# Another order of the steps of a twelve-block kernel: one string replaced, every instruction kept

## The chip, the cores and the metric

The kernel runs on one core of one Trainium2 chip. The time is the device time of one execution in microseconds. It computes with TensorE (PE), VectorE (DVE), ScalarE (ACT) and GpSimd (POOL); SyncE (SP) issues the DMAs. Each engine takes its instructions strictly in the order in which they were written, and waits at semaphores for the others.

## The reference

A residual stream `x` of 64 sequences x 64 tokens x 128 channels runs through four layers of three blocks (cross attention over a context of 128 x 96 per sequence, self attention, feed-forward), all in fp32:

```python
x = x + _L0_xattn_ref(_layernorm(x), ctx_768, ...)   # L0x
x = x + _L0_attn_ref(_layernorm(x), ...)             # L0a: linear attention and an MLP
x = x + _L0_ffn_ref(_layernorm(x), ...)              # L0f: 16 experts, top 4
x = x + _L1_xattn_ref(ctx_768, _layernorm(x), mask, ...)   # L1x
...                                                  # L1a, L1f, L2x, L2a, L2f, L3x, L3a
x = x + _L3_ffn_ref(_layernorm(x), ...)              # L3f: 8 experts, top 2, and a shared one
return x
```

## The kernel before

The stream stays in SBUF for the whole run (`x_held`, 32 tiles of 128 tokens). A block is cut into jobs by groups of four tiles (two for L1x and L2f). Two contexts (0 and 1), each with its own four PSUM banks, SBUF rooms and semaphores, work on two jobs at a time; `PLAN` says which jobs each context does and in what order. Both contexts share the five engines.

A job's work on one engine is a Python generator: what stands between two `yield`s is one step, with its waits in front (`wait_ge`) and its semaphore increments behind. Each generator has a letter. Main programs: `p`, `c`, `m`, `n` on PE; `a`, `b`, `x`, `y` on ACT; `g` on POOL; `v`, `r`, `w`, `z` on DVE; `s` on SP. Early programs, of the context's next job while the present one runs: `d` on DVE (norm statistics), `l` on POOL, `k` on ACT, `q` on SP (context load). Small letters are context 0, capitals context 1. `ORDER` is one string; `write_out` walks along it and writes the next step of each letter's program. The relative order of letters of different engines has no effect on the chip; that of one engine is the order of its queue. A `+` loads the weights of the next block on SP, after a wait for the jobs that used the same room.

A digit in front of a PE letter sets `job.warm`: `pe_warm` (L471) then issues that many matmuls of constants, 128x512 in bf16, ahead of the step's wait. Nobody reads them; here they are called fillers.

Lines that the argument uses: L904, L908 and L914 are the gate, up and shared matmuls of the expert blocks and L946 their down matmuls; L893 is POOL's product with the experts' weights; L1596, L1606, L1624 and L1699 are matmuls of the attention of L1a and L3x and L1726 its reduction on DVE; L1976 and L1984 are the scores and the transposes of L2x, L2081 and L2087 its maximum and subtraction on DVE; L400 and L436 are the norm statistics of the early programs; L2786 adds the last block's result and L2809 stores it to `out`.

Of the kernel before, what the change touches and what calls it, by code (L numbers as in the profile page):

```python
# [3091 lines left out]
```

## Time and profile before

| | us |
|---|---|
| median of 3 runs | 2549.42 |
| the runs | 2548.19 to 2553.82 |
| profiled execution, its own time | 2545.65 |
| its span, first to last instruction | 2544.3 |
| PE busy / weight loads (PEld) busy | 2247.8 / 1508.2 |
| DVE / ACT / POOL busy | 1746.2 / 1371.3 / 775.2 |
| mean granted TensorE clock | 0.971 of full |

The profiled execution is 1.35 us longer than its span (what lies around it) and 3.8 us shorter than the median of the runs. A busy time is the union of an engine's instructions; the fillers count as busy. The idle time of a stretch is its length less the busy time.

### The profile page before, as it was taken

How to read it: one execution, taken by the hardware profiler on the slowest of the kernel's cores; microseconds unless marked ns; L12 is line 12 of the kernel's file. 1: busy time of each engine (PE TensorE's matmuls, PEld its weight loads, DVE VectorE, ACT ScalarE, POOL GpSimd, SP SyncE). 2: the span in 40 equal slices, each digit the busy share in tenths (PEclk: the TensorE clock that was granted, in tenths of full speed). 3: DMA queues.
4: the chain of work that ended last, by engine and by line, in shares of the span. 5: the costliest groups of instructions: out<-in, count | busy, mean ns of one | idle time of the engine just before them, and what ended most of it. 6: DMA issues, size and time to landing. Idle time of an engine off the chain costs nothing.

```text
span 2544.3 us, 62025 instructions
## 1 busy us (share of the span) xinstructions
PE 2247.8 (88%) x26402; PEld 1508.2 (59%) x26526; DVE 1746.2 (69%) x4832; ACT 1371.3 (54%) x2286; POOL 775.2 (30%) x676
## 2 busy tenths in 40 slices
PE   5989999878988888997888888898887889999999
PEld 3557666655565555565655676665555556556666
DVE  5766766677667777676777777777767675555642
ACT  4766567654554666544567544344454544555542
POOL 3333546433342212121222123211123223224543
PEclk9999999998999999999999999999998999999999
DMA  3011313200000000010000000000000102211232
GB/s 116 19 42 35 80 46 75 47 19 9 9 11 14 9 8 6 1 47 11 17 16 10 20 25 25 25 11 17 17 11 16 58 8 55 57 56 55 55 105 63
DMA packets 50453, 84.14 MB, mean 33 GB/s; under 512 B 9537, under 2 KB 24769, under 8 KB 49793
## 3 DMA queue, kind: packets, MB, share of 16 engines
q1 hardware_dynamic: 50176, 80.18, 11.5%
q8 instruction: 208, 3.41, 0.6%
q14 instruction: 69, 0.56, 0.1%
HBM read 77.54 MB, written 2.62 MB: 32 GB/s over the span
## 4 chain that ended last, share of the span: by engine, by line
PE 61%; DVE 24%; ACT 8%; issue 3%; POOL 2%; DMA 1%; SPq 0%; another core or an unknown queue 0%; DVEq 0%; POOLq 0%; ACTq 0%
PE psum L946 6%; PE psum L908 5%; PE psum L904 5%; PE psum L1606 3%; PE psum L463 2%; PE psum L471 2%; PE psum L1984 2%; PE psum L1699 2%; DVE c_L2x_mx L2081 2%; DVE c_L2x_p L2087 1%; DVE c_L3x_most L1726 1%; PE psum L1395 1%; PE psum L1596 1%; PE psum L1976 1%; PE psum L778 1%
## 5 line engine op out<-in xcount | busy, mean ns | idle before, releaser
L893 POOL TENSOR_TENSOR c_L3f_h<-c_L3f_h,c_L3f_spread 128x512 f32<-128x512 f32 x96 | 121.3, 1290 | 157.9 <-DMA c_L3f_spread<-scratch 91.6
L471 PE MATMUL psum<-halves_held 128*128 128x512 bf16 x438 | 129.4, 409 | 17.5 <-issue 9.8
L936 DVE TENSOR_TENSOR c_L3f_h<-c_L3f_h,psum 128x512 f32<-128x512 f32 (+1 forms) x112 | 76.0, 684 | 88.7 <-PE psum L908 63.1
L922 ACT ACTIVATE c_L3f_h<-psum 128x512 f32<-128x512 f32 (+1 forms) x112 | 65.8, 596 | 124.1 <-PE psum L904 117.5
L946 PEld LDWEIGHTS psum<-weights,c_L3f_h 128*128 128x128 f32 (+1 forms) x896 | 106.5, 191 | 19.5 <-issue 15.0
L946 PE MATMUL psum<-weights,c_L3f_h 128*128 128x128 f32 (+1 forms) x896 | 111.3, 278 | 0.3 <-POOL c_L3f_h L893 0.3
L904 PE MATMUL psum<-c_L3f_xT,weights 128*128 128x512 f32 x208 | 107.2, 600 | 0.2 <-DVE c_L3f_h L936 0.2
L908 PE MATMUL psum<-c_L3f_xT,weights 128*128 128x512 f32 x208 | 107.1, 601 | 0.0
L893 POOL TENSOR_TENSOR c_L0f_h<-c_L0f_h,c_L0f_spread 128x512 f32<-128x512 f32 x64 | 83.9, 1335 | 43.8 <-DVE c_L0f_h L936 32.5
L2020 ACT ACTIVATE c_L2x_p<-c_L2x_p 128x1024 f32<-128x1024 f32 x64 | 67.6, 1057 | 54.1 <-DVE c_L2x_p L2087 54.0
L1606 PE MATMUL psum<-c_L3x_qx,c_L3x_kT 32*128 32x256 f32 x512 | 75.3, 417 | 22.9 <-DVE c_L3x_most L1726 17.5
L471 PEld LDWEIGHTS psum<-halves_held 128*128 128x128 bf16 x558 | 51.3, 102 | 73.9 <-issue 33.1
L2081 DVE TENSOR_REDUCE c_L2x_mx<-psum 128x8 f32<-128x1024 f32 x64 | 77.9, 1220 | 19.4 <-PE psum L1976 18.7
L893 POOL TENSOR_TENSOR c_L2f_h<-c_L2f_h,c_L2f_spread 128x256 f32<-128x256 f32 x64 | 45.4, 735 | 143.4 <-DMA c_L2f_spread<-scratch 137.9
L1984 PE MATMUL psum<-constants_held,c_L2x_p 128*128 128x128 f32 x512 | 72.3, 289 | 13.3 <-ACT c_L2x_p L2022 13.1
L1984 PEld LDWEIGHTS psum<-constants_held,c_L2x_p 128*128 128x128 f32 x512 | 61.3, 149 | 30.3 <-issue 16.6
L2087 DVE SCALAR_TENSOR_TENSOR c_L2x_p<-psum,c_L2x_mx 128x1024 f32<-128x1024 f32 x64 | 78.0, 1221 | 1.3
L1726 DVE TENSOR_REDUCE c_L3x_most<-psum 128x16 f32<-128x2048 f32 x32 | 73.2, 2287 | 6.7 <-PE psum L1596 6.3
L1606 PEld LDWEIGHTS psum<-c_L3x_qx,c_L3x_kT 32*128 32x128 f32 x512 | 44.9, 191 | 50.9 <-DVE c_L3x_most L1726 25.8
L2025 ACT COPY c_L2x_pT<-psum 128x1024 f32<-128x1024 f32 x64 | 64.1, 1009 | 18.7 <-PE psum L1984 18.6
L1976 PE MATMUL psum<-c_L2x_kx,c_L2x_qT 32*64 32x512 f32 x512 | 62.8, 615 | 10.5 <-DVE c_L2x_va L2062 6.2
L922 ACT ACT_TABLE_LOAD x55 | 70.6, 1283 | 1.0
(640 smaller groups left out, 6514.1 us busy)
## 6 DMA issues: line engine op xcount, KB each, us to landing
c_L0f_spread<-scratch SPq DMA_DIRECT2D x64, 256.0 KB, 5.5
c_L3f_spread<-scratch SPq DMA_DIRECT2D x32, 512.0 KB, 5.5
c_L2f_spread<-scratch SPq DMA_DIRECT2D x64, 128.0 KB, 3.0
c_L3f_spread<-scratch SPq DMA_DIRECT2D x64, 128.0 KB, 5.9
c_L0x_ctxT<-ctxT SPq DMA_DIRECT2D x8, 384.0 KB, 7.7
c_L1x_ctx<-ctx SPq DMA_DIRECT2D x16, 192.0 KB, 2.4
c_L2x_ctxT<-ctxT SPq DMA_DIRECT2D x8, 384.0 KB, 3.6
c_L3x_ctxT<-ctxT SPq DMA_DIRECT2D x8, 384.0 KB, 3.6
```

The costliest lines, as they stand in the source:

```text
L471: nc.tensor.matmul(j.psum[:, bank, :], j.half["ident"], j.half["take"], start=True, stop=True)
L893: nc.gpsimd.tensor_tensor(h, h, j.m["spread"][:, f, :], ALU.mult).then_inc(*j.up("mixed"))
L904: t.matmul(psum[:, 1 + 2 * f % 3, 0:j.tok], j.weight("gate")[:, cols], m["xT"][:], start=True, stop=True).then_inc(*j.up("gate"))
L908: t.matmul(psum[:, 1 + (2 * f + 1) % 3, 0:j.tok], j.weight("up")[:, cols], m["xT"][:], start=True, stop=True).then_inc(*j.up("inner"))
L922: nc.scalar.activation(j.m["h"][P - rows:P, f, :], j.psum[0:rows, 1 + 2 * f % 3, 0:j.tok], ACT.Silu).then_inc(*j.up("silu"))
L946: put = nc.tensor.matmul(j.psum[:, 0, k * P:(k + 1) * P], j.m["h"][rows, f, k * P:(k + 1) * P], j.weight("down")[rows, f * P:(f + 1) * P], ...
L1606: nc.tensor.matmul(j.psum[rows, g, at:at + 256].rearrange("p (j q) -> p j q", j=QUAD), j.m["kT"][f, s * keys:(s + 1) * keys], j.m["qx"][f, ...
L1726: put = v.tensor_reduce(m["most"][:, u, :].rearrange("p (g j) -> p g j", j=QUAD), psum[:, :, u * QUAD * keys:(u + 1) * QUAD * keys].rearra ...
L1976: put = t.matmul(psum[64 * r:64 * r + 64, g, :].rearrange("p (j k) -> p j k", j=QUAD), m["qT"][f, s * S:(s + 1) * S], m["kx"][f, :, s * SC ...
L1984: put = t.transpose(psum[:, n // 4, (n % 4) * P:(n % 4 + 1) * P], m["p"][:, n * P:(n + 1) * P], j.c["ident"])
L2081: v.tensor_reduce(mx, s, AX, ALU.max).then_inc(*j.up(lane_name("max", h)))
L2087: v.scalar_tensor_tensor(p, s, -limit, bcast(mx, 2, SC), ALU.max, ALU.subtract).then_inc(*j.up(lane_name("low", h)))
```

## The change

The string `ORDER` is replaced by another of the same 8123 steps. The letters' counts are equal; the sum of the digits is 558 before and 590 after; they stand in front of 178 PE steps before and 189 after. `PLAN`, the programs, the tiles and every instruction except the fillers are the same. The first two, the 22nd and 23rd, and the last lines of the strings:

```diff
@@ -2838,76 +2838,76 @@
     "a2a3a4a5a6a7b3b4b5b6b7c3c4c5c6c7d8d9dadbdcdddedfe4e5e6e7f4f5f6f7g4g5g6g7h4h5h6h7i8i9iaibicidieifj4j5j6j7k5k6k7l6l7")

 ORDER = (
-    "vdDqDddldkqQdddplVDaL2pDaKQDdDDPpPagA1pgApLkpvGvD3PaAGvvVvpPaPKPg1paVAd5pagVdVdVPpAppvPlAlvda4PDAGQPGkvd5PvvD1PkVDpLVaAd"
-    "dDdvvlavdpavvaK1pVVvVP1PAApvvGkPvAlvG3PvQvvdPgPVvV9pgADDaDLaaVVaVPppppDapAppKDDDLDpQvvpPaAapaPaKpAPkdvvdvvdlGGvdlpvvPvPv"
...
-    "vAgpVKPpAPVPAvvvpPPAaPADqGPADVdpVADddvGvvalVavvVvGvvvvvvvvvvvvvLVp1PvaVDvpvAvPPdApAPapVvVpApvaVgVKppkvgPaApVaPvgpApvPgpV"
-    "+DPpVADp2PvvPVvVqpVVGPapPVGvVApVDvLagPv1pVaVPg3PdnAPzmAzzPwy6nwwAdPyVny2nVxVPdzlzV2mVG1nxVmzxmwzw3mzPyw7PwwAnxP3mynxymnx"
...
-    "PSPASpVPPAapVvpaGbPsLPAGPVDpvGsPaGApsVPGvPAsGPVPASgCVgCsPPASPVPApVCCpPpAGaPvGPVpAgaPKgPVvPGACVgPpGCaGACVgCCGCgCgCCCVSPpA"
-    "pPaPRvPRRgBRRpRRpRARvCgPBaSpApvSVPgPVSpAaPSvPVgPASGPVPAGPVGPAPGVPAGPVPGAPVGPAGPVPAGPVPGApVpGapvPaPvAPVPGAPVcAVcccccccccc"
-    "cccCvsCCCCCCCCCCCCCVS")
+    "dDddDDLDlqkKppaaPApaPAppp3PdqQDdvDQDddldLVggkGvDvaAGvvVvpPaPPgpaV3pAdagVdVVPpApKpvdPAlvaDdl2PAG5PkGv3PvdvDPDVpkQLVaDAddd"
+    "vvlva3plavvaKpVVvVPA3PApDDvvPGvAddvPvGvv2PgPvVQV8pAaaVVVPpppADapaLapgDpkppGKvDDvpPaAvaQv1pvaPvaAG2pkdddDPLvDlplvvdPvPvVk"
...
+    "gKpVPgAVpKPApPvVPPAvAvpPDADPaAdDGVddPqvAvpVGvaaVvVlvDvvvvvvvvvvvvGvvvVLpVDav1PvPAApvPvAKpaPVVpApVaVpvpgvapgPaApvdpVvgpPg"
+    "ApPVVpPDADpv2Pkv+PVPPvVVpVvVGaqppGVVDALvavPd1pgaVGnVPPzAzzPmwywAw3nAPPynyVVnVzzDPVxmVnxVmxmzwwz3mzPwwy7PwdA1nPxymnxymnxz"
...
+    "pVrrpVaVpVrpvDGapVpdvadpVPvApVrarpPbrPrArrApVcVbPvGAppGVaPsaPGKldPvvVPAppsAagAPgAsPgVcgcAcsgpgAPPsgPpAccaPcpPpappkpapapG"
+    "pKDVvVVVVvVVVVvDvvgpaVvpgVaDpVLcvPgVcgVcVgVcGcpVacvcVPVAcvVspaPApPAPGVArprapGVPrbPGDrrrvPrKVprPApPRRraPRRRpDBRpRvRPRDAPC"
+    "VAPVPApBcaaPVPvDAPbpvPVAPsVPSPpaPpvpapSAvpVGaPALPVASPsGVPGDAPVPGsApGpGPVPgvASPgVpPgASPagVCvgCGPpGapGCKAGPVCGCGCCCPACVCCc"
+    "CCCVvSPApapvPRRBRPRRRRPRRPACABpapvpVaPSVPAPVPAPVPAPSVpGPAPGVPGAPVPsSAPGVPAGPVPSgApgPVPSgvAPagVPsAcgPVGccGPGAcGccgPGVPcGC"
+    "GpgpaCAVCvCvCCCccCCCCCccccvCCVsS")
```

The last lines of the new string hold, for instance, `CCCccCCCCCccccvCCVsS` where the old one ends in `cccccccccccccCvsCCCCCCCCCCCCCVS`: the down steps of the two last L3f jobs alternate. In the 23rd line the first `n` (the first scores of L2x in context 0) stands ahead of two steps `P` of L1a instead of behind them.

## Rows read from the trace of the kernel before

**Rows 1.** The page's totals, and the span with the mean granted clock.
```profile
PE 2247.8 (88%) x26402; PEld 1508.2 (59%) x26526; DVE 1746.2 (69%) x4832; ACT 1371.3 (54%) x2286; POOL 775.2 (30%) x676
...
core 0: 2544.3 us, clock 0.971
```

**Rows 2.** Four stretches: busy us and instructions of each engine, PE's clock, DMA share, GB/s.
```profile
0.00:127.00 127.00, 95.79 (x641) 59.44 (x650) 84.34 (x252) 75.77 (x124) 45.32 (x40) 0.99 0.22 68
127.00:509.00 382.00, 354.23 (x2356) 246.64 (x2359) 255.62 (x935) 250.31 (x467) 172.21 (x137) 0.99 0.23 54
509.00:2162.00 1653.00, 1422.11 (x20511) 963.87 (x20624) 1204.78 (x3129) 861.60 (x1417) 414.88 (x386) 0.96 0.06 18
2162.00:2544.00 382.00, 375.71 (x2910) 238.24 (x2899) 201.49 (x520) 183.67 (x280) 142.82 (x113) 1.00 0.23 65
```

**Rows 3.** The same view, of the fillers (L471) alone, two stretches.
```profile
127.00:509.00 382.00, 2.72 (x8) 1.51 (x15) 0.99 0.23 54
509.00:2162.00 1653.00, 114.53 (x391) 45.30 (x496) 0.96 0.06 18
```

**Rows 4.** Chain that ended last: shares by engine, and by line.
```profile
PE 61%; DVE 24%; ACT 8%; issue 3%; POOL 2%; DMA 1%; SPq 0%; another core or an unknown queue 0%; DVEq 0%; POOLq 0%; ACTq 0%
...
by line: PE psum L946 6.4%; PE psum L908 5.2%; PE psum L904 5.1%; issue 3.3%; PE psum L1606 2.8%; PE psum L463 2.1%; PE psum L471 1.8%; PE psum L1984 1.7%; PE psum L1699 1.6%; DVE c_L2x_mx L2081 1.6%; DVE c_L2x_p L2087 1.3%; DVE c_L3x_most 
```

**Rows 5.** Who PE waited for: us in total, times, longest us.
```profile
PE psum L552 <- DMA c_L0x_ctxT<-ctxT: 22.0, 1, 22.0
```

**Rows 6.** Timeline 783 to 790: start us, us, engine, line, work, [idle before, releaser].
```profile
782.39 1.22 DVE L1726 TENSOR_REDUCE c_L1a_most<-psum 128x16 f32<-128x1024 f32 x1
783.09 0.69 ACT L480 ACTIVATE c_L2x_qT<-psum,weights 128x512 f32<-128x512 f32 x1 [2.74 <-PE psum L1897]
...
783.65 2.00 PE L1606 MATMUL psum<-c_L1a_qx,c_L1a_kT 32*64 32x256 f32 x24 [0.60 <-DVE c_L1a_most L1726]
...
785.57 0.87 DVE L400 BATCH_NORM_STATS2 c_L2x_norm_stats<-x_held 128x6 f32<-128x128 f32 x4
...
787.40 1.08 PE L1976 MATMUL psum<-c_L2x_kx,c_L2x_qT 32*64 32x512 f32 x4
...
788.99 1.23 DVE L2081 TENSOR_REDUCE c_L2x_mx<-psum 128x8 f32<-128x1024 f32 x1 [2.55 <-PE psum L1976]
```

**Rows 7.** Busy time of the engines from 783 to 795.
```profile
783.00:795.00 12.00, 9.92 (x158) 5.07 (x166) 8.77 (x19) 5.34 (x6) 2.12 (x2) 0.78 0.01 1
```

**Rows 8.** Timeline of PE from 1376 to 1381.
```profile
1377.02 2.78 PE L471 MATMUL psum<-halves_held 128*128 128x512 bf16 x8 [0.22 <-issue]
1379.63 1.58 PE L1984 MATMUL psum<-constants_held,c_L2x_p 128*128 128x128 f32 x13
```

**Rows 9.** The fillers: durations in ns (min/median/max), and their group (busy us, mean ns).
```profile
L471 PE MATMUL psum<-halves_held x438: 376/379/634, 25.6 to 2098.3; 128*128 128x512 bf16 x146
...
L471 PE MATMUL psum<-halves_held 128*128 128x512 bf16 x438 | 129.4, 409 | 17.5 <-issue 9.8 <-DVE c_L2x_p L2087 6.2
```

**Rows 10.** Timeline from 2499 to the end.
```profile
2499.21 0.19 PEld L908 LDWEIGHTS psum<-c_L3f_xT,weights 128*128 128x128 f32 x1 [0.24 <-issue]
...
2499.64 0.19 PEld L904 LDWEIGHTS psum<-c_L3f_xT,weights 128*128 128x128 f32 x1 [0.24 <-issue]
...
2515.52 25.75 PE L946 MATMUL psum<-weights,c_L3f_h 128*128 128x128 f32 x224
...
2528.42 0.69 DVE L2786 TENSOR_TENSOR x_held<-x_held,psum 128x512 f32<-128x512 f32 x1 [11.38 <-PE psum L946]
...
2541.31 0.69 DVE L2786 TENSOR_TENSOR x_held<-x_held,psum 128x512 f32<-128x512 f32 x1 [12.21 <-PE psum L946]
```

**Rows 11.** Weight loads on SP (to landing), and two starts, at 1693 and 1811.
```profile
DMA to landing us min/median/max: 2.6/4.3/11.4
...
1693.15 0.47 PE L2299 MATMUL psum<-c_L2f_klT,c_L2f_qlT 32*64 32x128 f32 x16
...
1811.18 0.87 DVE L436 BATCH_NORM_STATS2 c_L3a_norm_stats<-x_held 128x6 f32<-128x128 f32 x4
```

More of the change, by code:

```diff
@@ new lines @@
+    "AVlPVApVdApaPapVapaPVVkpVVpVpVVpvGvpVaG4pbPrrArprrrprrrrPdAPdrdrPKlPALADrPrArrPrrrrPaPVvVPcApbaVVAPsAVpVAppaPpsapPKDdDvv"
+    "DLVgVsgvpVVgDcVs+cVKgVcVapGspVcvPGApLpPgAPAPAPAPPaPavDPVgkVPpApaVVAPAVcVAcvpKDgvPgcVcvPVpVaVVpbVpVVrpraGpaVpv1PDGDArprrL"
+    "arrPrrLPdrrADPDrArrPArAvdPdrrrrPKrlPPcVbVPAppasPAAppApsaPpapsPKDDVVvVDVdLvLgVgvVgVcVsgcVpVgVsaVpGccVvcPvGApgapvgPDAPgPkP"
+    "AAPAPPKPVVPAcDA1PAcAcVVVVvpaPpbppaPpappKDDdVrrrrrrrdrrvrVrrrVdvrlrpaVpvrapVrdrpvDrrapcVVVbpvaGppLVavpsPGDApapPAPAPskPAgA"
@@ new lines @@
+    "PsgPKdPgvPsVgcvgcVsqcPDgDAdcgdcPlBcgdRRcdRRRcRRRDPRAvRPLPkdRVDRRPdRpRRaRPRdpqvapvRRAApVC+BaapgPalvSPVgPKvvAPVdAPVPAPgSVP"
+    "vAPGPppSvaVAPapGdVaSGCCGpSGCvGvCCGavCkGCvCVPdAdpavPlDBDdpdRaRRPRRpRkvpRadPRRpRRavpRRRpRRRdAdRRaRlapVPgaCvBgPAvPvVAPVdPSk"
+    "PgqAPvApvpadpaddDaPVlVSpPvGvPSGavdCLvPSA1pGavPGVkSpGaPApAGVdvppaaGDpvdapagqvpPaVCdgKCvGvCCCCgvCpvdpapaldaV1PkddApdvlv2PP"
+    "avPvdPBDRpRavRRRRRApRdaRRRPVpkvpapdvRaRRpdADDdaRpRRLaRVqRgpRvCaBPgAPlvvPVdAPdSdPVdAPgvPpvApaVpaaPSVpGPvvlPSaPvGvCSApGdad"
@@ new lines @@
+    "vCkSGCkGpAaCGpvppadDddaPvlVpVapGdqdKdGdapgCavCgCvvCVPADD1PgBPvRvDPR1pARpRaRLpaRRRaPlVARRRpkRPvRvdRPVRDRPaRRvRPRCvABVpavP"
+    "kpAaS3pvpavPddpddapldapVAgSvKpaGPaSGVPAdPgvPSGvAPVddCSqCgPvlApvpapaGdaPkGpGCvvVCVaCvGCvkpGavCpa2pvppdadddavplapagqpCaVPA"
+    "gvvdvPBdPddDPAQPgAPvlkpvRpdaRpRaVad3pPvvPVDRRRavPvRRRApaAvRPRRRRpkRDaVLpVvppavadpddDaRRpRRlRaDDgdpvDPaCBPgAvPvAVPKVPSPgP"
+    "v2pvpapaaAASVpPvGvSGaCvLCvSpGavCGDSkVpGDapGvCpdvGaCGpKpvCvCvCvVppgdPPVAgdVvPvPvQaAApAG+PvgAplvD2pGVaVDVpaapGVpdvvvV3pv7P"
@@ new lines @@
+    "AvpvDkpLPDaPADDApaPpaVVpAvvvDvVLVD9pDvpaPdKpVpKvAvPvAvPVg2PDApgPvPpvvdQadAlApPGAvgPvDDpVpALVaGpVVDaDDDappGvLVvdvD4pvk9Pv"
+    "pvV2pPaPAAApaPapVVpAvvvvDV9pVvpaPKVppKvApvPvAvPV1PgPDADAgvPvPpvdQadAVDApGLPgvDApvKV2pGaVVDdpDaapGVpvDvvLv3pl7PvpvdpVPaPA"
+    "AApaPapVVpAvvvkvVVD7pDvpaPdpVKApvPAvv2PvV1PPAgDDAppgvPvPvVDQaLAgpGvDPpKvAVpdaDApGaVVaDpDpvGvvLV4pv3PvdpvPlVpaPAAApaPapVV"
+    "pAvvvvDdVV9pkv1PApVadvvKvvpdaavPvvAvvv1PvvvVPPAvdvvAvvPvlvvDdPDpDDvaVvLADQAPpGvAvVGkVpVDaDpapGvDVpLVpPPgDAPvaAApgKpavPKp"
@@ new lines @@
+    "zdmwAwnlAPgzPKVzVV6mVz4PwwwVPAPyPPVnxVVymPVnVGdxDmDGxy2mVnwwzkVDzmLw2nwAwPzzxz9myVxV6nmyPxnmywPwnzAzpaPApvAdpdPaPvdqplVV"
+    "PvpVaV4pgaVGnVPPzmAzzdPAwDwPwyx8nAmyPnxyVnzzmVKVxVn1mzwz1PwzVPAm2PwyPVwnwynVPPVxyVVGmnDzzGxVnmVAzzx7mzwPw1myV1nwPwynwynV"
+    "zzDD3PxnLAmzgxPmAxmwAwz3mzPPwDwyw1nVVVx1PVymnxyVmnxVz2mzwwkpPaPApvKdpddPaAqpApPavPv2pgVaVlVmVnGwdw1PwzzzVPA2PPxPPV3myVx1"
+    "nVmVyxVGnmDyDwG2nwzzVnVA1mzPwzwzwyV7nxPVDPyLAmnGxmgxy1mw1nwzzkmPwwnAwPAPzzxz8mVVDVyPVxnmyxVnmyVPwnwzPzAmPwwAnwPAzPzxV6mz"
@@ new lines @@
+    "KVVVy2PxVnmy1PxnAy2m+wnVwzzDPDVpVAVaAVVVVV1pVVVVVVVDVvpVVaVpPpavApvPagVVVLVnVDmzzKPAzPwwPywAVPnGxPyVmndydGdxPAmnAzxzPmww"
+    "nVmzGPwzPzPVwPwGyPVxVVPnAmyDxDDVVPVmALAVnxVyV2mVlwnwVzzVVV1mVnwVwwzzxzdVVVVVVVV8mVPyA2nxPVmyxnmywVwkPAmnwzzwPAnwPzzxPzVP"
+    "VmGyAGPxnAgmyxPnyPmnzwwzPVpVaPGDpGvPKvpddadPVlVvVPAapvaDvVa2PvVVADAVVVVVVdVVVV6pVvVVVDVVVpPvVLvAVvPVpkaPpvpadAdPVvavpvaP"
+    "AVvPGPAVaPGPAVpGPvDPVpKvGdPvlvdPPpVaVVPA2pDkVvVPVpAAdVaVVVQVVVVVVVVVVVVV7pVVPAPVvvaavPVADDvPdadAPldVpGvPLAPVDpvvGvPAPpVa"
@@ new lines @@
+    "PVGkPpGKvpadPdPPVVvvpaVadVvlavlPDdDDdApvPpvGPvAv1pVa+QPAVpkvNpMapapYappXNagMYLNXkdZZZvWWWvvvvvvdMgXYpg2MNZZWWGdppppv7Nva"
+    "vpvMaZaWZpZpvvWvYvpvvNDvpvvK1pWYvNgYvvgvl8pXlaprrprbrrMrNrrrXvdrrrrrZcabMXpvpka1MpvsWpZWapMNWpWdapvspgWavsgcgcZgZcvcXcZv"
+    "paMpavapXppYvMvaXNgvYvpvMWWNgY1MgNZZpWWpWppvX3NkvaZvZpva2MaZpYpvXvNvvpYvMvXvNYMWNWZpZvPvA1pvPgvvgvdVPpAa2prrpdrbrrPGPrar"
+    "prrArprrarrdPcvvlbpvdppkaVAsVQNMZZpvapsZpgvasgvcgcWgcDcDWcYWvpaNYpavpXapMvvpXNgYMvlXNavMZZWWgvD2NMgZZpLpZpWDWpYWpvX6NvdY"
```

96 lines of the change are left out of this document (33 added, 63 removed).

## The prediction

> **What bounds the kernel now.** I read the totals first [rows 1]: TensorE (PE) is busy 2247.8 us of a 2544.3 us span, VectorE (DVE) 69%, nothing else over 54%. Those are averages, so the second view is the table of stretches [rows 2]. The reader should subtract PE's busy time from each stretch's length: 0 to 127 us leaves 31.2 us idle, 127 to 509 leaves 27.8, 509 to 2162 leaves 230.9, and the last 382 us leave 6.3. In 509 to 2162 DVE is busy 1204.8 of 1653 us (73%), so two engines take turns at being late; at both ends PE is alone. Third, the fillers: `pe_warm` (L471) issues matmuls nobody reads while PE would wait. They are counted as busy: 129.4 us in all, 114.5 of them in 509 to 2162 [rows 3, 9]. So PE did no useful work for 230.9 + 114.5 = 345.4 us there, and for 27.8 + 2.7 = 30.5 us in 127 to 509. Fourth, the chain that ended last [rows 4]: PE 61%, DVE 24%, and the fillers themselves 1.8% of 2544.3 = 46 us. What an order of steps can win is in that pool of idle and filler time. It can't win the first wait, 22.0 us for the context's DMA [rows 5]: the SP queue of the new string has the same first eight steps.
>
> **What the change is, counted in the strings.** Every letter is one step of one engine's program in one of the two contexts; only the order within one engine, and the digits (fillers ahead of a PE step), reach the chip. Both strings have the same 8123 steps. I split them by engine and compared the k-th with the k-th. PE: 539 of 2448 steps stand elsewhere; a smallest set of 204 moved steps explains it, all but 39 of them by at most three places. DVE: 635 of 3306 moved (317 are early steps `d`, the norm statistics of the next job; 265 are `v`). ACT 202 of 1520, POOL 102 of 664, SP 17 of 185. Fillers: 558 before, 590 after. PLAN, buffers, tiles, banks and instructions are the same, so the useful busy time of each engine should stay.
>
> **Part 1: swaps on PE, 509 to 2162.** By the start times of the trace, about 302 of some 1550 PE steps there (19.5%) stand elsewhere. If the lost time is spread evenly over the steps, 0.195 x 345.4 = 67 us of it lies where PE's order changes; in 127 to 509 it is 54 of 395 steps, 0.137 x 30.5 = 4 us. How much of it comes back I take from one place worked [rows 6]. Before: the matmul L1606 of L1a waits for the DVE reduce L1726 and starts at 783.65; the first scores L1976 of L2x (step `n`) stand two steps behind it and start at 787.40, though their input was written by ACT at 783.09 + 0.69 = 783.78. DVE then sits idle 2.55 us until it can start its reduce L2081 at 788.99. After: `n` stands ahead of L1606's step, and one early `d` (the four L400, 0.87 us) stands ahead of the DVE step L1726. By hand: L1726 and what follows is 0.87 later, `n` starts near 783.8, DVE is free near 785.6 + 0.9 = 786.5 and starts L2081 there, 2.5 us sooner. One context gains 2.5 and the other loses 0.9, so 1.6 net for the pair if both are needed. In 783 to 795 PE was idle 12.0 - 9.9 = 2.1 us and had 2.7 us of fillers [rows 7], so a third of 4.8 us comes back. This place was chosen because its gain is plain; others move a step behind a wait for no reason that I can see, such as one up matmul that now goes behind the L1984 of 1379.63, in front of which 2.78 us of fillers ran [rows 8]. I take a quarter of the lost time: (67 + 4) / 4 = 18 us. Ends: nothing (each saving is waited away at the next shared engine) and a half, 36 us.
>
> **Part 2: fillers.** 32 more. Those on the chain now cost 46 us over 558 = 0.08 us each, so +2.6 us. Ends: 0 (each lies inside a wait) and 32 x 0.409 = 13 us [rows 9]. A sum of fillers that rises by 6% also doesn't look as if PE's waits at these points became shorter.
>
> **Part 3: early steps on DVE.** No step is added. 402 of the moved ones stand earlier and 210 later; a mean DVE step is 1746.2 / 3306 = 0.53 us. Moved ahead of a step that PE waits for, it costs its length; moved out of the way, it gives it back. The surplus of 192 x 0.53 = 101 us matters where DVE is on the chain, 24% of it: at most 24 us, and nothing where DVE idles anyway. I take +3 us, near the lower end, since DVE idles 27% of the stretch.
>
> **Part 4: the granted clock.** The mean is 0.971 over the span and 0.96 in 509 to 2162 [rows 1, 2]; a filler takes 379 ns at the median and 634 at the longest, the latter at the lower of the two levels, 1.2 GHz [rows 9]. That mean is about 0.04 x 1653 = 66 us of full clock lost, at most. The change re-deals where PE pauses, and a tenth of that either way is 7 us. I take 0. The stretch from 2162 on has the full clock with no fillers at all, on PE's own work. The Trainium skill ("TensorE: Matmul & The Clock Gate", What's actually happening) says that the throttled clock is the default and activity releases it; by that rule more fillers give a little back, perhaps the same 7 us, and the trace agrees as far as that last stretch goes.
>
> **Part 5: the last 382 us.** Here the new string differs most: 175 of 421 PE steps stand elsewhere, one of them by 42 places, since the last two L3f jobs interleave their gate, up and down matmuls instead of running them in blocks. PE is busy 375.7 of 382 us [rows 2], and from 2515.5 on it runs 224 down matmuls in 25.75 us without a pause [rows 10]. The same matmuls in another order take the same time: 0, ends -3 and +3. The two stores to `out` come closer together (the first DVE addition was 12.9 us ahead of the last), which adds at most the store's own 2.3 us after 2542.0. [...]
>
> **Part 6: SP.** The weight loads move; the largest move puts L3a's load behind steps that ran at about 1693, and L3a's first step ran at 1811.2; a weight load lands in 11.4 us at most, so it stays hidden [rows 11]. The other exchanges on the queue are of a context load with an expert's spread, none by more than seven places once the weight loads are left out. I take 0; ends 0 and +3.
>
> **The sum.** -18 + 2.6 + 3 + 0 + 0 = -12.4 us against the profiled execution's own 2545.65 us, which is 2533. The median of the three runs is 3.8 us above that execution, so the forecast on the median's scale is 2549.4 - 12.4 = 2537 us. Its own range, from a gain of 5 to one of 22, is 2527 to 2544.
>
> **The rivals.**
> (a) No gain. Each swap only exchanges which context waits, because PE and DVE together are the bound in the middle and the last 382 us can't move. For it: the filler sum rises; 92% of PE's steps aren't in the moved set. Against: 345 us of lost time is much to find nothing in. Time: 2549, within 5.
> (b) Slower: DVE as the bound of 509 to 2162. Early `d` steps stand ahead of a step for which PE waits, and on one in-order queue PE's wait grows by each one's length. Without Part 3 the sum is -15.4 us, so it decides from 15.4 / 0.53 = 29 of the 317 moved `d` steps on the chain; with 50 of them it is +11: 2560. For it: more steps moved earlier than later. Against: DVE idles 27% of that stretch.
> (c) Slower by the clock: PE's pauses fall so that the lower clock is granted for half as long again; 33 us, of which PE's share of the chain, 61%, is 20 us. Against the forecast's 12 that is 2557. Nothing in the strings says which way it goes; the fillers speak against.
> (d) Half of the lost time at the moved steps comes back: 36 of the 71 us, less 6 for Parts 2 and 3: 2519. For it: the place worked gave a third.
> (e) The change doesn't do what it says: the strings might differ between letters only across engines, which changes nothing on the chip. The count by engine excludes it.
>
> **How the numbers follow.** Forecast's case 0.46; (d) 0.14; (a) 0.20; (b) 0.11; (c) 0.09. What this kernel's measurement can tell from no change is about 0.2%, 5.1 us. Faster 0.60, the same 0.20, slower 0.20. The range reaches from just past (d), 2516, to 2557, which takes in (a) and about half of (c) and leaves out (b) and the far side of (d).
>
> **What would show it.** Right: in 509 to 2162 (some 10 us shorter) PE's idle plus filler time falls from 345 to about 333 us; L2081's idle time waiting for L1976 falls; the last 382 us keep their busy time; DVE's busy time stays at 1746 us. Wrong: the idle time falls but the fillers take it over; the mean clock moves by 0.005 or more and explains the result by itself; DVE's share of the chain rises past 30% (rival b); or the gain sits in the first 509 us or the last 382.

## The result and the profile after

| | before | after |
|---|---|---|
| median of 3 runs, us | 2549.42 | 2570.69 |
| the runs | 2548.19 to 2553.82 | 2568.83 to 2571.73 |
| profiled execution, its own time | 2545.65 | 2568.83 |
| its span | 2544.3 | 2567.5 |

The ratio is 1.0097, 95% interval 1.0072 to 1.0121: about 25 us slower (the two medians are 21 us apart, the two profiled executions 23). Measured again beside the experiments on another chip it is 1.0105 (1.0086 to 1.0124). The forecast was 2537 us, the range ended at 2557, and slower had a chance of 0.20.

The totals and the clock of after answer to [rows 1], the chain to [rows 4]:

```profile
PE 2260.2 (88%) x26429; PEld 1513.9 (59%) x26558; DVE 1749.9 (68%) x4832; ACT 1369.3 (53%) x2286; POOL 777.7 (30%) x676
```
```profile
core 0: 2567.5 us, clock 0.970
```
```profile
PE 58%; DVE 26%; ACT 9%; issue 3%; POOL 2%; DMA 1%; SPq 1%; another core or an unknown queue 0%; DVEq 0%; ACTq 0%; POOLq 0%
```

Nothing in the totals explains 23 us. DVE is busy 3.7 us more, the clock is the same, and no engine's share of the chain moves by more than 3 points. The stretches answer to [rows 2], the last line, of the fillers alone in the middle, to [rows 3]:

```profile
127.00:509.00 382.00, 346.74 (x2272) 241.11 (x2282) 246.08 (x907) 245.76 (x456) 165.92 (x134) 0.97 0.23 53
509.00:2162.00 1653.00, 1420.15 (x20466) 961.01 (x20575) 1205.50 (x3124) 859.79 (x1421) 421.70 (x390) 0.96 0.06 18
2162.00:2567.50 405.50, 396.92 (x3098) 254.66 (x3097) 211.67 (x557) 190.83 (x291) 147.32 (x116) 0.99 0.22 62
```
```profile
509.00:2162.00 1653.00, 120.26 (x416) 47.88 (x524) 0.96 0.06 18
```

From 127 to 509 PE is busy 7.5 us less than before. In the middle its idle plus filler time is 1653 - 1420.15 + 120.26 = 353 us, where 333 were forecast and 345 stood before. Both traces lack a part of the filler records (391 of 496 and 416 of 524 are there). In later traces that have all of them the sum is 352.5 us for the old order (b_sp_moved), 357 for the old order with the new digits (b_a_digits), and 368 for the new order (after_again).

Since both kernels have the same steps, the useful table is made by matching them: for each PE step, its start after less its start before, as the median of 20 us of steps up to the time named.

| time in before, us | 60 | 275 | 300 | 430 | 460 | 500 | 1340 | 2130 | 2215 | 2270 | end |
|---|---|---|---|---|---|---|---|---|---|---|---|
| after is late by, us | 1.2 | 3.8 | 8.4 | 7.3 | 14.2 | 14.2 | 13.3 | 19.5 | 20.4 | 23.6 | 23.2 |

So 14 of the 23 us are lost by 460 us, in jumps, the middle to 1340 gains nothing, and the rest comes after it, 3 us of it in one jump near 2250. One pair of traces is a rough measure, though: between 1180 and 1220 us the execution of before was itself some 4 us longer than most others of the old order (last section), which hides as much in the middle. What a stretch costs is therefore taken from the times of the experiments, and the traces say only where to look. The jump of 275 to 300, on DVE, then on SP, then on PE:

```profile
276.79 0.86 DVE L417 SCALAR_TENSOR_TENSOR c_L0f_norm_shift<-c_L0f_norm_moments,c_L0f_norm_rstd 128x4 f32<-128x4 f32 x1
288.34 0.74 DVE L400 BATCH_NORM_STATS2 c_L1x_norm_stats<-c_L1x_ctx 128x6 f32<-128x96 f32 x4 [10.69 <-DMA c_L1x_ctx<-ctx]
288.99 0.67 DVE L936 TENSOR_TENSOR c_L0f_h<-c_L0f_h,psum 128x512 f32<-128x512 f32 x1
289.58 0.68 DVE L828 TENSOR_TENSOR c_L0a_xin<-c_L0a_xin,psum 128x512 f32<-128x512 f32 x1
...
290.78 0.85 DVE L831 TENSOR_TENSOR x_held<-x_held,c_L0a_xin 128x512 f32<-128x512 f32 x1
```
```profile
275.52 5.12 SPq L865 DMA_DIRECT2D c_L0f_spread<-scratch  x8
280.68 0.59 SPq L1163 DMA_DIRECT2D c_L1x_ctx<-ctx  x1
```
```profile
285.76 2.84 PE L946 MATMUL psum<-weights,c_L0f_h 128*128 128x128 f32 x24
291.73 1.09 PE L463 MATMUL psum<-constants_held,c_L0f_xn 128*128 128x128 f32 x4 [3.12 <-issue]
```

The early step `d39` (norm statistics of L1x's context, 0.74 us) holds DVE's queue for 10.69 us, because its load was issued at 280.68, behind eight DMAs of an expert's spread, and landed 7.7 us later (the median landing of this load is 2.4 us). L828 and L831 (`V105` and `V106`), which end in `x_held`, stand behind it. PE's L463 at 291.73 has to wait for the semaphore `done` that L831 raises, and it starts 0.1 us behind L831's end at 291.63; that is read from the program, the profile names no releaser ("issue"). The two other traces of the new order's start, after_again and a480_then_b, show the same wait of `d39`, 10.24 and 10.06 us. It also happens to `d93` (4.05 us here, 3.24 and 3.57 there):

```profile
444.17 0.74 DVE L400 BATCH_NORM_STATS2 c_L1x_norm_stats<-c_L1x_ctx 128x6 f32<-128x96 f32 x4 [4.05 <-DMA c_L1x_ctx<-ctx]
```

Here PE loses more than DVE waits, 6.9 us in the table for 4.05. It idles 1.81 us for L936 and 2.08 us for L1368, both behind `d93` on DVE, and behind these waits it runs at a granted clock of 0.50. Two windows of after behind the waits, then the stretch around these steps in before:

```profile
448.00:452.00 4.00, 2.45 (x9) 2.10 (x10) 2.44 (x3) 1.48 (x4) 4.00 (x4) 0.59 0.00 0
452.00:456.00 4.00, 4.00 (x42) 2.58 (x41) 0.82 (x1) 2.26 (x4) 1.58 (x2) 0.56 0.00 0
```
```profile
428.00:448.00 20.00, 19.42 (x138) 13.85 (x136) 13.04 (x26) 12.13 (x28) 15.44 (x12) 1.00 0.39 84
```

In before `d39` ran without any wait, behind L828 and L831:

```profile
282.53 0.69 DVE L828 TENSOR_TENSOR c_L0a_xin<-c_L0a_xin,psum 128x512 f32<-128x512 f32 x1 [7.49 <-PE psum L778]
283.25 1.27 DVE L831 TENSOR_TENSOR x_held<-x_held,c_L0a_xin 128x512 f32<-128x512 f32 x1
...
285.34 0.72 DVE L400 BATCH_NORM_STATS2 c_L1x_norm_stats<-c_L1x_ctx 128x6 f32<-128x96 f32 x4
```

Two changes meet: on SP `q2` and `q8` (the loads) stand behind `s11` to `s14` and `S18`, `S19` (spreads), and on DVE the steps that use them, `d39` and `d93`, stand earlier.

### The profile page after: what moved, and what is told of

The parts are those of the page before. It is cut to its first block, busy times and chain, and to the rows that moved or that the text cites. A ratio compares the mean times of both kernels' runs of the same rounds, so it can differ in the third digit from the quotient of the medians.

```text
span 2567.5 us, 62086 instructions
## 1 busy us (share of the span) xinstructions
PE 2260.2 (88%) x26429; PEld 1513.9 (59%) x26558; DVE 1749.9 (68%) x4832; ACT 1369.3 (53%) x2286; POOL 777.7 (30%) x676
## 4 chain that ended last, share of the span: by engine, by line
PE 58%; DVE 26%; ACT 9%; issue 3%; POOL 2%; DMA 1%; SPq 1%; another core or an unknown queue 0%; DVEq 0%; ACTq 0%; POOLq 0%
PE psum L946 6%; PE psum L908 5%; PE psum L904 5%; PE psum L1606 3%; PE psum L463 2%; PE psum L1699 2%; PE psum L471 2%; DVE c_L2x_mx L2081 1%; PE psum L1984 1%; DVE c_L3x_most L1726 1%; DVE c_L2x_p L2087 1%; PE psum L1596 1%; PE psum L1395 1%; PE psum L1976 1%; PE psum L778 1%
## 5 line engine op out<-in xcount | busy, mean ns | idle before, releaser
L893 POOL TENSOR_TENSOR c_L3f_h<-c_L3f_h,c_L3f_spread 128x512 f32<-128x512 f32 x96 | 121.5, 1292 | 176.1 <-DMA c_L3f_spread<-scratch 108.2
L471 PE MATMUL psum<-halves_held 128*128 128x512 bf16 x463 | 133.9, 402 | 16.6 <-issue 10.0
L936 DVE TENSOR_TENSOR c_L3f_h<-c_L3f_h,psum 128x512 f32<-128x512 f32 x112 | 75.3, 683 | 84.2 <-PE psum L908 66.6
L946 PEld LDWEIGHTS psum<-weights,c_L3f_h 128*128 128x128 f32 (+1 forms) x896 | 107.0, 191 | 19.1 <-issue 15.6
L908 PE MATMUL psum<-c_L3f_xT,weights 128*128 128x512 f32 x208 | 107.4, 601 | 0.0
L471 PEld LDWEIGHTS psum<-halves_held 128*128 128x128 bf16 x590 | 53.8, 102 | 77.5 <-issue 36.5
L893 POOL TENSOR_TENSOR c_L2f_h<-c_L2f_h,c_L2f_spread 128x256 f32<-128x256 f32 x64 | 46.1, 740 | 149.0 <-DMA c_L2f_spread<-scratch 140.5
L893 POOL TENSOR_TENSOR c_L0f_h<-c_L0f_h,c_L0f_spread 128x512 f32<-128x512 f32 x64 | 83.1, 1324 | 26.4 <-DVE c_L0f_h L936 18.3
L2081 DVE TENSOR_REDUCE c_L2x_mx<-psum 128x8 f32<-128x1024 f32 x64 | 77.8, 1219 | 14.5 <-PE psum L1976 14.0
L1976 PE MATMUL psum<-c_L2x_kx,c_L2x_qT 32*64 32x512 f32 x512 | 63.0, 617 | 14.5 <-DVE c_L2x_va L2062 7.4
```

The lines of the kernel that those rows point to most:

```text
L471: nc.tensor.matmul(j.psum[:, bank, :], j.half["ident"], j.half["take"], start=True, stop=True)
L893: nc.gpsimd.tensor_tensor(h, h, j.m["spread"][:, f, :], ALU.mult).then_inc(*j.up("mixed"))
L908: t.matmul(psum[:, 1 + (2 * f + 1) % 3, 0:j.tok], j.weight("up")[:, cols], m["xT"][:], start=True, stop=True).then_inc(*j.up("inner"))
L946: put = nc.tensor.matmul(j.psum[:, 0, k * P:(k + 1) * P], j.m["h"][rows, f, k * P:(k + 1) * P], j.weight("down")[rows, f * P:(f + 1) * P], ...
L1976: put = t.matmul(psum[64 * r:64 * r + 64, g, :].rearrange("p (j k) -> p j k", j=QUAD), m["qT"][f, s * S:(s + 1) * S], m["kx"][f, :, s * SC ...
L2081: v.tensor_reduce(mx, s, AX, ALU.max).then_inc(*j.up(lane_name("max", h)))
```

## The experiments

A step is named by its letter and its number among that letter's steps. Every kernel computes all of the reference. Each ratio is against the kernel before, measured on the same chip. "The place at 1340 to 1380" means how much later PE's steps get between these two times of before, taken from the two traces.

### The two late loads

The first theories were three. Theory 1: this pair, the wait for a late load in DVE's queue. Theory 2, rival (b): the length of the early steps. Theory 3, rival (c): clock and fillers. First the new order with either half of the pair undone, then the old order with the SP half alone. In a_dve_back `d93` stands further back than in the old order, where it was ahead of `V138` and `V139`.

```diff
 SP queue, new order (run a_sp_back)
-s11 s12 s13 s14 q2      ...  S18 S19 q8
+q2 s11 s12 s13 s14      ...  q8 S18 S19
```


> The new order with one thing undone: on SP two context loads of L1x (jobs 0 and 6, each one load of the context and two of the mask) stand again ahead of the expert spreads of L0f behind which the new order put them. All other queues as in the new order. Theory 1 (a context load that is issued behind a spread lands some 8 us after its issue instead of 2.4, and an early norm step placed early on DVE then blocks that queue, 10.7 and 4.05 us in the trace of the new order): both stalls shrink to about nothing, and the time falls by the 4.7 + 6.8 us that the two places cost, from 2570.7 to about 2560. Theory 2 (DVE is delayed by the length of early steps put ahead, SP's order is harmless): 2570, within 2. Theory 3 (the granted clock, 0.970 against 0.971, or the 32 more fillers): 2570, within 2.

```diff
 DVE queue, new order (run a_dve_back)
-d39 v81 V105 v82 V106 D53      ...  d93 v147 v148 V139
+v81 V105 v82 V106 D53 d39      ...  v147 v148 V139 d93
```


> The new order with another thing undone: on DVE the two early norm steps of L1x that wait for these context loads (the statistics of the context of jobs 0 and 6) stand again a few steps later, behind the steps of L0f, L0a and L1x that they blocked. SP as in the new order. Theory 1: the loads land as late as before, but nothing that PE needs stands behind the waiting step, so most of the 11.5 us comes back: 2560 to 2563. Theory 2 (length of early steps in general): the two steps are 0.74 us each, so at most 1.5 us: 2569. Theory 3: 2570.

```diff
 SP queue, old order (run b_sp_moved)
-q2 s11 s12 s13 s14      ...  q8 S18 S19
+s11 s12 s13 s14 q2      ...  S18 S19 q8
```


> The old order with only these two context loads moved behind the spreads on SP. DVE as in the old order, where the two steps that wait for them stood at 285.3 and 434.0 us. Theory 1: the loads land at about 285 and 436, so the steps wait 0 to 3 us each, and the time is 2551 to 2554: the late load alone is nearly harmless, it is the pair that costs. If SP's order alone were the cause: 2549 + 11 = 2560. Theories 2 and 3: 2549.

| run | ratio (95%) | late by at 300 / 460 us |
|---|---|---|
| a_sp_back | 1.0072 (1.0049 to 1.0095) | 2.1 / 2.4 |
| a_dve_back | 1.0049 (1.0032 to 1.0066) | 2.6 / 3.0 |
| b_sp_moved | 1.0002 (0.9988 to 1.0016) | 0.3 / 2.1 |

Either edit removes both jumps: 8.4 and 14.2 us become 2 to 3, and in neither trace does the granted clock fall at 448 us. In a_sp_back the load is issued ahead of the spreads and the step runs at once:

```profile
272.94 0.42 SPq L1163 DMA_DIRECT2D c_L1x_ctx<-ctx  x1
273.41 1.26 SPq L1166 DMA_DIRECT2D c_L1x_mask<-mask  x2
274.71 3.85 SPq L865 DMA_DIRECT2D c_L0f_spread<-scratch  x6
```
```profile
276.22 0.72 DVE L400 BATCH_NORM_STATS2 c_L1x_norm_stats<-c_L1x_ctx 128x6 f32<-128x96 f32 x4
```

By its time the SP half alone costs nothing that can be measured (4 us at most by the interval), since in the old order the step that needs the load comes later: `d39` had no wait. `d93` waited 2.2 us, and in that trace PE's steps get 1.9 us later between 430 and 460. So it is the pair: a later load and an earlier user. Theory 2, the length of the early steps, falls with a_dve_back, which moved two of them and gained some 0.5% against after_again (1.0105, on another chip). a_dve_back had the higher clock too (0.975), so its time says more than the jumps. The time of a_sp_back says less: 1.0072 is 2568 us on the scale of the median before, where theory 1 had 2560 and the others 2570, and its interval reaches up to that of after_again. So that the late load matters is shown by the jumps in the traces, and by a_dve_back's time; what the pair costs lies between the 0.33% and the 0.56% by which the two runs are below after_again.

### Where the loss lies: the new order in one stretch at a time

```diff
 every engine's queue; each stretch is cut where both orders have written the same steps
-old order from 0 to the end
+old to 480 us, new from there        (b_then_a480)
+new to 480 us, old from there        (a480_then_b)
+new only between 480 and 1340 us     (b_a480_1340)
+old to 1340 us, new from there       (b_then_a1340)
+new only between 1340 and 2130 us    (b_a1340_2130)
+old to 2130 us, new from there       (b_then_a2130)
```


> The old order on every queue up to about 480 us of the old trace, the new order from there (fillers as well). In the new order's trace PE's steps were 14.6 us late at that point and 23 us at the end. If the losses are local and add up: 2549 + 8 or 9 = 2558. If the early part's loss is a shift that later slack would have swallowed: 2565 or more. If most of the 21 us comes from the middle or the end after all (a late start only hid it): 2570.

> The new order up to about 480 us, the old one from there. Theory of two places (two context loads that land late hold VectorE's queue, 3.8 + 6.8 us and about 2 us at the start): ratio 1.0040 to 1.0050, about 11 us, and nothing added after 480 us. Rival (the loss is spread evenly over the changed steps, 480 of 2545 us): 1.0018.

> The old order, with the new one only between about 480 and 1340 us. Theory of places: the traces show +2.1 us at 820 to 860 us and gains and losses of about 1 us elsewhere, so ratio 1.0005 to 1.0015. Rival (the remaining 0.53% is spread evenly from 480 us to the end): 860 of 2065 us, so 1.0022.

> The old order up to about 1340 us, the new one from there. Theory of places: +2.3 at 1340 to 1380, +1.8 at 1420 to 1460, +1.6 at 1500 to 1540, -1.4 at 1860 to 1900, +2.6 at 2220 to 2260 us, -0.9 after 2500: about +6 to +9 us, ratio 1.0024 to 1.0035. Rival (spread evenly): 1205 of 2065 us of 0.53%: 1.0031; so the first half tells them apart, and here the place of VectorE's step of 0.7 us (V839) beside GpSimd's product, which should take over 2 us again.

> The old order with the new one only between about 1340 and 2130 us, the half of the last part (1.0035 from 1340 us on) that holds the places at 1340 to 1380, 1420 to 1460, 1740 to 1780 and 1860 to 1900 us. Theory of places: 1.0015 to 1.0022. Rival (the loss lies in the stretch where TensorE alone is the bound, after 2160 us): 1.0005 or less.

> The old order up to about 2130 us, the new one from there: the rest of the last part. Theory of places: +0.8 at 2140 to 2180 and +2.6 at 2220 to 2260 us (V839 at 2.3 to 2.8 us), -0.8 at the end: 1.0010 to 1.0015. Rival (the last stretch is the loss): 1.003 or more. My prediction of this stretch was 0 us, with ends of 3.

> The changed kernel itself, beside the other three, to have its ratio from the same chip. All theories: 1.009 to 1.010 times the kernel before.

| new order in | ratio (95%) |
|---|---|
| everything (after_again) | 1.0105 (1.0086 to 1.0124) |
| 0 to 480 | 1.0047 (1.0031 to 1.0063) |
| 480 to the end | 1.0053 (1.0036 to 1.0069) |
| 480 to 1340 | 1.0007 (0.9994 to 1.0020) |
| 1340 to the end | 1.0035 (1.0020 to 1.0049) |
| 1340 to 2130 | 1.0028 (1.0015 to 1.0042) |
| 2130 to the end | 1.0024 (1.0012 to 1.0036) |

The four stretches add up: 0.47 + 0.07 + 0.28 + 0.24 = 1.06% for 1.05%. Each has an interval of 0.12 to 0.16% to either side, so a coupling across them of more than some 0.35% is excluded, a smaller one isn't (1340 to the end is 0.35% in one piece and 0.52% in two). And the loss isn't spread evenly: a third of the kernel, from 480 to 1340, costs next to nothing, the first 480 us nearly half of it all. The last stretch costs 6 us (3 to 9) where I had 0 with ends of 3. It and 1340 to 2130 cost more than their places in the traces gave (1.0010 to 1.0015, and 1.0015 to 1.0022).

### Single moved steps

Comparing the traces in windows of 40 us showed the same places in the traces of the new order and not in those of the old. Three were tried in the old order, together and then apart.

```diff
 PE queue, old order (b_three_moves; b_n48 has the first of these alone)
-p484 p485 p486 N48 M48
+p484 N48 p485 p486 M48
-P448 p511 p512 c51
+P448 c51 p511 p512
 ACT queue (b_three_moves; b_b27 has this alone)
-A459 b27
+b27 A459
```


> The old order with three steps moved ahead as the new one has them: on TensorE N48 ahead of p485, c51 ahead of p511; on ScalarE b27 ahead of A459. Theory of places (a moved step waits where it now stands, and what stood there loses its slot; GpSimd's product starts earlier and meets VectorE's step V839): +1.8 us at 1340 to 1380, +1.6 us at 1420 to 1460, +2 to +3 us at 2220 to 2260 us with V839 at 2.3 to 2.8 us in place of 0.73; together +5 us, ratio 1.0015 to 1.0022. Rival (single moves cost nothing by themselves, the loss comes from many moved steps together): each place within 0.5 us of the kernel before, ratio 1.0000.

> The old order with one step moved: b27 (ScalarE, the squares from which the expert's spread of c_L3f is made) ahead of A459. Theory (GpSimd's product starts some 1.6 us earlier and runs when V839's four small VectorE instructions come): V839 2.3 to 2.8 us in place of 0.73, +3.1 us at 2220 to 2260 us, ratio 1.0008 to 1.0014. Rival (V839 is longer but the kernel has slack behind it): ratio 1.0000 to 1.0004.

> The old order with one step moved: N48 (TensorE, cross attention's scores) ahead of p485 and p486. It waits 3.0 us with nothing of TensorE beside it. Theory: +3.2 us at 1340 to 1380 us, 10.2 us at the lower granted clock behind the wait (3.4 in the kernel before), ratio 1.0008 to 1.0014. Rival (the 3.2 us come back where TensorE waits for VectorE anyway): 1.0000 to 1.0003.

| run | ratio (95%) | place 1340 to 1380 | 1420 to 1460 | 2220 to 2260 |
|---|---|---|---|---|
| b_three_moves | 1.0027 (1.0014 to 1.0041) | +3.2 | +0.1 | +3.1 |
| b_b27 | 1.0013 (1.0001 to 1.0026) | 0.0 | 0.0 | +2.8 |
| b_n48 | 1.0016 (1.0003 to 1.0029) | +3.7 | 0.0 | 0.0 |

Three steps of 8123 cost 0.27%, a quarter of the whole loss, and two of them carry it. The third, `c51`, was a miss: PE idles 1.15 us for it (DVE's L2457) where `p511` and `p512` used to run, and all but 0.2 us of it comes back at the next wait. In the whole new order the two others cost less in the traces than alone: 1.2 and 1.4 us at 1340 to 1380 (after and after_again), and at 2220 to 2260 the 3 us of after are 0.2 in after_again.

**b27.** It makes the input of an expert's spread, so GpSimd's product L893 starts sooner against `V839`, by 1.6 to 2.3 us in eight of the nine traces with this move. In before the four small DVE instructions of `V839` come ahead of it:

```profile
2246.11 0.19 DVE L1732 CAST c_L3x_top<-c_L3x_most 128x16 bf16<-128x16 f32 x1
2246.33 0.17 DVE L1734 TENSOR_TENSOR c_L3x_rest<-c_L3x_most,c_L3x_top 128x16 f32<-128x16 f32 x1
...
2247.84 3.71 POOL L893 TENSOR_TENSOR c_L3f_h<-c_L3f_h,c_L3f_spread 128x512 f32<-128x512 f32 x3 [27.08 <-DMA c_L3f_spread<-scratch]
```

In b_b27 they run beside it:

```profile
2242.09 2.48 POOL L893 TENSOR_TENSOR c_L3f_h<-c_L3f_h,c_L3f_spread 128x512 f32<-128x512 f32 x2 [24.88 <-DMA c_L3f_spread<-scratch]
2242.55 0.84 DVE L1732 CAST c_L3x_top<-c_L3x_most 128x16 bf16<-128x16 f32 x1
2243.43 1.18 DVE L1734 TENSOR_TENSOR c_L3x_rest<-c_L3x_most,c_L3x_top 128x16 f32<-128x16 f32 x1
...
2244.99 0.10 PEld L1659 LDWEIGHTS psum<-halves_held,c_L3x_top 128*128 128x128 bf16 x1 [1.42 <-DVE c_L3x_top L1737]
```

Instructions of 0.19 and 0.17 us take 0.84 and 1.18; the first ends near the end of one GpSimd product, the second near the end of the next, and L1659 on PE waits 1.42 us. `V839` took 0.73 us in all traces without this move and 2.3 to 2.8 in eight of the nine traces with it. In after_again GpSimd's product began only 0.64 us behind `V839`'s start, and `V839` took 0.74; so the move makes the meeting likely, and a few tenths of a microsecond decide. (a_six_back, below, has it moved back.) The Trainium skill ("SBUF — State Buffer", Who interferes with whom) says that VectorE and GpSimd share one port pair under an exclusive lock, and that a VectorE instruction with two SBUF inputs contends with a GpSimd one that reads SBUF. The trace agrees for L1734, which has two such inputs and ends with GpSimd's second product, and for L1735, which has two as well, starts at 2244.53 as that product ends (2244.57), and takes 0.18 us. L1732 has a single input; for that the section wants one of VectorE's two-port modes, and no run here shows whether it ran in one.

**N48.** In its new place as in the old one it starts 3.26 us behind `p484`, when DVE (L2062) lets it; but `p485` and `p486`, which ran inside that wait, now run behind it. PE idles 2.66 us instead of 1.80:

```profile
1363.99 1.98 PE L1976 MATMUL psum<-c_L2x_kx,c_L2x_qT 32*64 32x512 f32 x8 [2.66 <-DVE c_L2x_va L2062]
1365.90 1.22 PE L908 MATMUL psum<-c_L2f_xT,weights 128*128 128x256 f32 x2
...
1367.91 1.98 PE L1976 MATMUL psum<-c_L2x_kx,c_L2x_qT 32*64 32x512 f32 x8
```
```profile
1364.00:1374.00 10.00, 10.00 (x31) 4.95 (x32) 6.86 (x23) 4.21 (x11) 0.00 (x0) 0.50 0.00 1
```

The second fence is the window behind the wait: PE is busy all of it, at a granted clock of 0.50 (1.2 GHz), and L908 takes 1.22 us. The lower clock lasts 10.2 us here and 3.4 us at this place in before. Is the price the slot or the clock? The same move was run with fillers in the wait.

```diff
 PE queue (b_n48_filled)
-p484 N48 p485 p486 M48
+p484 9N48 p485 p486 M48
```


> As b_n48, with 9 fillers ahead of N48, so that TensorE works in that wait. If the price of the move is the clock that falls behind the wait: no 10.2 us at the lower clock there, the place costs +0.8 us at most, ratio 1.0000 to 1.0004. If it is the slot that p485 and p486 lose (0.8 us of work, and what waits behind it): as b_n48, +2 to +3 us, 1.0008 to 1.0012.

```profile
1369.96 1.09 PE L1976 MATMUL psum<-c_L2x_kx,c_L2x_qT 32*64 32x512 f32 x8 [2.67 <-DVE c_L2x_va L2062]
1370.98 0.70 PE L908 MATMUL psum<-c_L2f_xT,weights 128*128 128x256 f32 x2
```
```profile
1370.00:1380.00 10.00, 9.06 (x48) 4.54 (x49) 7.50 (x23) 7.65 (x14) 0.00 (x0) 1.00 0.14 38
```

In its trace the clock stays at 1.00 and the place costs 0.4 us instead of 3.7. Its time, though, is 1.0022 (1.0007 to 1.0038), no better than b_n48. So the trace says that most of the place is the clock behind the wait, and the times don't confirm it: I had expected 1.0004 at most if it were the clock and 1.0012 at most if it were the slot. This stays open.

### Fillers and the clock

```diff
-digits of the old string, 558 fillers
+digits of the new string on the old order, 590 fillers      (b_a_digits)
+no digits, no fillers                                       (b_no_fillers)
```


> The old order with the new one's digits: 590 fillers for 558, at 150 steps another number. Rival of the fillers: 250 differences of 0.235 us, of which the 32 more alone are 7.5 us, stand ahead of ready steps: ratio 1.003. Theory of places: fillers mostly stand in waits, and the digits that suit other places cost at most half of their 7.5 us: ratio 1.0000 to 1.0015, with the granted clock within 0.003 of the kernel before.

> The old order with no fillers at all (558 before). If fillers cost their share of the chain, as Part 2 of the prediction priced them (0.08 us each), 46 us come off: 0.982. If they pay for themselves by the clock that they hold up: the granted clock falls from 0.971 to 0.94 or less and the time rises by 1% or more. In between, the mean clock says which part is which.

b_a_digits is 1.0000 (0.9987 to 1.0014): the 32 more cost nothing. b_no_fillers is 1.0290 (1.0266 to 1.0314), 74 us slower, with a mean clock of 0.915; in the middle the granted clock is 0.88 where it was 0.96 [rows 2]:

```profile
509.00:2162.00 1653.00, 1365.87 (x19606) 948.40 (x19605) 1170.40 (x3011) 835.44 (x1370) 394.33 (x369) 0.88 0.05 16
```

Rival (c), a lower clock over the whole kernel, falls as the cause: after and before have the same clock to 0.001, and b_then_a480, with 0.975, is still 0.5% slower. Behind single waits the clock does fall, as at 448 us above.

### The place that the prediction worked

Between 783 and 790 us the other executions of the old order were 1.3 to 1.7 us shorter than the one I had read, with nothing changed there. In the traces it is the granted clock: 0.78 in the window of [rows 7], and in the same steps of b_b27, whose order there is the old one:

```profile
787.40:799.40 12.00, 9.84 (x245) 5.46 (x247) 9.65 (x21) 5.94 (x8) 1.75 (x2) 1.00 0.01 3
```
```profile
791.30 1.22 DVE L2081 TENSOR_REDUCE c_L2x_mx<-psum 128x8 f32<-128x1024 f32 x1 [0.85 <-PE psum L1976]
```

L2081's idle time is 0.85 us here, where [rows 6] has 2.55. So the moves of exactly that place were made in the old order:

```diff
 PE queue (b_hand)
-P293 P294 n0 P295 m0 P296 n1
+n0 P293 P294 P295 m0 n1 P296
 DVE queue
-V257 V258 d143
+d143 V257 V258
 ACT queue
-A205 y0
+y0 A205
 fillers: the new order's at this place, 10 fewer (548 for 558)
```


> The old order with the new one only at the place that the prediction worked (n0 ahead of P293, n1 ahead of P296, d143 ahead of V257, with the digits there). The prediction: 1.6 us gained, ratio 0.9994, with the first scores L1976 2.9 us and the reduce L2081 3.0 us sooner. Theory now (the idle time read there came from the lower clock of that one execution): the steps after n2 stand within 0.3 us of an execution of the old order that had the full clock there, ratio 1.0000 to 1.0004.

Its ratio is 1.0001 (0.9986 to 1.0016). Starts of four steps, counted from the start of `p339`, the last step ahead of the place:

| us from p339 | n0 (L1976) | first L2081 | n2 | P299 |
|---|---|---|---|---|
| before, clock 0.78 there | 10.1 | 11.7 | 18.8 | 26.5 |
| b_b27, old order, clock 1.00 | 8.8 | 10.0 | 17.1 | 24.7 |
| b_a_digits, old order, new fillers | 9.0 | 11.1 | 19.1 | 26.8 |
| after | 8.1 | 9.6 | 17.9 | 25.8 |
| b_hand | 6.9 | 8.5 | 19.1 | 27.0 |

The moves do bring the scores and the reduce forward, by 3.2 and 3.1 us against before, nearly as worked out. By `n2` nothing of it is left: against the old order at the full clock after is 0.8 us late and b_hand 2.1. But b_hand took the new order's fillers along, and b_a_digits, which has these and the old order, is as late at `n2` and `P299`. So with the same fillers the moves bring the reduce forward by 2.5 us and neither gain nor lose anything by `n2`; the 2.1 us go with the ten missing fillers. The moves with the old fillers weren't run. In both traces the clock falls there. In b_hand PE idles 1.9 us ahead of `n0` (for GpSimd's L2039), and behind that, in the window 790 to 800 us, the clock is 0.52 with PE busy 9.31 us; in the same window of b_a_digits it is 0.58:

```profile
790.00:800.00 10.00, 9.31 (x128) 4.99 (x119) 5.86 (x12) 5.24 (x6) 0.00 (x0) 0.52 0.01 2
```

My theory's bound of 0.3 us for b_hand was a miss; the time shows no change, but couldn't tell the 1.6 us of the prediction from nothing.

### Six steps put back in the new order

```diff
 new order (a_six_back)
+q2 ahead of s11, q8 ahead of S18           (SP)
+N48, M48 behind p486; c51 behind p512      (PE)
+b27 behind A459                            (ACT)
```


> The changed kernel with six of its moved steps put back: q2 and q8 (SP, loads of the context) ahead of the expert's spread; N48 and M48 behind p486, c51 behind p512 (TensorE); b27 behind A459 (ScalarE). Theory of places: 1.0105 less 0.0033 to 0.0047 for the two loads and 0.0020 to 0.0027 for the others: 1.003 to 1.005. Rival (in the new order other waits take their place, the loss is of the whole order): 1.007 or more, no better than the loads alone put back (1.0072).

The ratio is 1.0056 (1.0038 to 1.0075), where after_again has 1.0105, though on another chip: six moved steps account for about half of the loss. It is just above what I expected (1.003 to 1.005) and below what the rival did (1.007 or more); its interval reaches into both. In the trace `d39` has no wait again, `V839` takes 0.73 us, and the place at 1340 to 1380 costs 0.4; the one at 1420 to 1460 still costs 1.8, so `c51` was never its cause. For the other half the traces show further places of 1 to 2 us, each a group of moved steps that wasn't taken apart: 1.7 at 60 to 100 us, of which 0.7 comes back, 1.8 at 1420 to 1460, and 0.8 at 2140 to 2180 in all but a_dve_back. They add up to 3.6 of some 14 us. So where most of the other half is lost isn't shown.

## Why the prediction was wrong

**Part 1 (-18 us)** failed, and with it the sign. Its size came from one place, and what I read there as room, DVE's 2.55 us of idle time ahead of L2081, was mostly that execution's lower clock (0.85 us in b_b27): the row with 0.78 stood in [rows 7] and I used only its busy time. PE's own idle and filler time was about the same at either clock, 4.8 and 4.4 us. That a third of it comes back was wrong: the moves bring the reduce forward as worked out, and in the traces nothing is left of it by `n2`; the time shows no gain (b_hand, 1.0001), within 4 us. The next step failed too, that lost time at moved steps comes back in a fixed share: the stretch from 480 to 1340 us, with 137 of 758 PE steps elsewhere, changed by 0.07% (the interval reaches from a gain of 1.5 us to a loss of 5), and 1340 to 2130 lost 7 us. The idle plus filler time rose instead of falling to 333. L2081's idle time for L1976 fell from 18.7 to 14.0 us in after, as listed under right, but it is 18.6 in after_again, and 16.7 in b_sp_moved, of the old order: this sign says nothing from one trace.

**Part 2 (+2.6)** was near, as a sum: the 32 fillers cost 0 (b_a_digits, within 3.6 us). Its unit price of 0.08 us was wrong in sign as an average, since all 558 together save 74 us.

**Part 3 (+3)** had the right suspect and the wrong price. I charged an early `d` step its length, 0.53 us. What two of them cost was their wait for a load, 10.69 and 4.05 us on DVE, and PE lost 4.6 and 6.9 us in the jumps at 300 and 460, the second time with the lower clock behind the wait. The count was no basis either: which steps count as moved depends on which smallest set of 635 is taken. One such set has 437 steps that stand earlier and 198 later, another 224 and 411, so a surplus like the 192 isn't a property of the change. Rival (b), that PE waits for DVE because early `d` steps stand ahead, is right in sign and short in size (2560, measured 2571), and by another mechanism and in another stretch: it needed 50 steps in the middle, and two ahead of 509 us did a third to a half of the loss. DVE's share of the chain rose by only 2 points.

**Part 4 (0)** held: 0.971 and 0.970. Only the sum is 0; single places of 3 us turn on it. (The stretch from 2162 us on has one filler, not none.) The rule of the Trainium skill that I cited, that activity releases the clock, agrees with b_no_fillers (0.915 without fillers); the gain of 7 us for more fillers that I worked out from it did not show.

**Part 5 (0, ends -3 and +3)**: PE did keep busy (8.6 us idle of 405.5, 6.3 of 382 before), and the alternating down steps cost nothing that I can see. But from 2130 us on the new order loses 6 us (1.0024, 3 to 9 us), at or outside my end of 3, about half of it by a step of DVE that got longer (2.71 us in that trace).

**Part 6 (0, ends 0 and +3)**: the weight loads stayed hidden. The exchanges that I named and set to 0, "a context load with an expert's spread", are half of the cause of the largest loss. Alone they cost nothing measurable (b_sp_moved), as I said; I didn't ask who uses the load and whether that user had moved as well. Parts 3 and 6 were priced one by one, and the loss is their product.

The range left out what happened because its upper end was drawn by the clock's rival, and because the costs on single queues were capped at 3 us each.
